# Two dense layers of a graph network in one stage, with part of the rounding on another engine

## The reference

```
edge_feat = gelu((x[src] + edge_attr) @ W_pre + b_pre) * bases
aggr = segment_sum(edge_feat, dst, num_segments=50000)
y = x + aggr
h = relu(batch_norm(y @ W1 + b1, g1, be1))      # mean and variance over all 50000 nodes
h = relu(batch_norm(h @ W2 + b2, g2, be2))
x = layernorm(x + y + h)                         # x + y = 2 (x + aggr / 2)
```

## Time and profile before

| what | value |
|---|---|
| median of 3 runs | 2237.25 us (2236.58 to 2238.08) |
| the profiled execution, its own time | 2248.79 us |
| its span (first to last instruction) | 2247.0 us |
| TensorE, weight loads, VectorE, ScalarE, GpSimd busy | 72%, 58%, 74%, 61%, 58% |
| DMA read and written | 332.27 MB, 295.04 MB, 279 GB/s over the span |
| statistics L500, mean of one | 0.688 us, 392 times |
| relu L780, mean of one | 0.809 us, 196 times |
| weight and instruction queues q8, q14 | 31 and 38 packets, 0.82 MB |

### The profile page before, as it was taken

One profiled execution on the slowest core, in us unless ns is written; L12 is line 12 of the kernel. 1 busy time (PEld: TensorE's weight loads), 2 busy tenths in 40 slices (PEclk: granted clock), 3 DMA queues, 4 the chain that ended last, 5 costly groups with the idle time before them and its releaser, 6 DMA issues. The chain is left out here.

```text
span 2247.0 us, 29418 instructions
## 1 busy us (share of the span) xinstructions
PE 1609.5 (72%) x7554; PEld 1295.5 (58%) x7554; DVE 1666.1 (74%) x3358; ACT 1365.9 (61%) x1981; POOL 1313.1 (58%) x1204
## 2 busy tenths in 40 slices
PE   2645569999996888994333333332599999999994
PEld 2434448888884655663232233232488778888884
DVE  2646646666667888996999999998377667777673
ACT  1322325555775766773888888887266656666663
POOL 5543147770006887001999999999446666666653
PEclk8877879999998999997555555555799999999997
DMA  9999759998879999995999999997412111212110
GB/s 341 368 347 352 260 161 340 342 340 316 289 249 285 342 339 342 344 325 232 385 397 399 401 404 400 395 407 308 169 37 67 63 62 57 65 63 64 55 53 32
DMA packets 171831, 572.69 MB, mean 255 GB/s; under 512 B 27441, under 2 KB 50583, under 8 KB 170322
## 3 DMA queue, kind: packets, MB, share of 16 engines
q1 hardware_dynamic: 123282, 445.99, 52.3%
q0 software_dynamic: 47136, 73.04, 13.8%
q10 hardware_dynamic: 1344, 52.84, 6.3%
HBM read 332.27 MB, written 295.04 MB: 279 GB/s over the span
## 5 line engine op out<-in xcount | busy, mean ns | idle before, releaser
L968 PE MATMUL d_pN<-k_ident,d_r 128*128 128x128 f32 x784 | 191.6, 425 | 337.2 <-ACT d_r L983 336.5
L968 PEld LDWEIGHTS d_pN<-k_ident,d_r 128*128 128x128 f32 x784 | 153.0, 222 | 375.9 <-issue 343.9
L500 DVE BATCH_NORM_STATS2 k_stats<-d_pH 128x512 f32 (+1 forms) x392 | 253.2, 688 | 100.8 <-PE d_pH L52 91.7
L991 ACT ACTIVATE d_o<-d_u,d_nb,d_rs 128x256 f32<-128x256 f32 x392 | 203.6, 590 | 81.2 <-POOL d_nb L1027 81.2
L1034 POOL TENSOR_TENSOR d_u<-d_x,k_base 128x1024 f32<-128x1024 f32 x98 | 230.9, 2356 | 14.6 <-DVE d_x L1059 9.5
L590 POOL DMA_INDIRECT scratch_y<-k_sums,k_target x98 | 151.9, 1550 | 120.7 <-POOLq L61 69.1
L50 PE MATMUL d_pH<-d_r_h,k_w_h 128*128 128x512 f32 x392 | 164.3, 419 | 57.3 <-DVE d_r_l L829 27.5
L780 ACT ACTIVATE d_r<-d_h,d_coef 128x512 f32<-128x512 f32 x196 | 149.2, 809 | 87.0 <-DVE d_r_l L829 41.8
L637 ACT ACTIVATE d_y_h<-d_pT 128x1024 fp32r<-128x1024 f32 x98 | 100.5, 1025 | 157.2 <-PE d_pT L606 133.1
L811 POOL DMA_INDIRECT scratch_y<-k_sums,k_target x98 | 175.0, 1786 | 33.3 <-issue 21.8
L530 POOL TENSOR_TENSOR bn_rstd<-bn_var,k_minus_half 128x2 f32<-128x2 f32 x2 | 1.5, 726 | 318.3 <-DMA d_h<-scratch_h 176.7
(11 more groups left out here) (201 smaller groups left out, 4960.1 us busy)
## 6 DMA issues: line engine op xcount, KB each, us to landing
d_y<-scratch_y SPq DMA_DIRECT2D x196, 512.0 KB
scratch_h<-d_h SPq DMA_DIRECT2D x196, 512.0 KB
d_h<-scratch_h SPq DMA_DIRECT2D x196, 512.0 KB
scratch_y<-in_x ACTq DMA_DIRECT2D x25, 2000.0 KB
scratch_x<-d_x SPq DMA_DIRECT2D x97, 512.0 KB
out<-d_o SPq DMA_DIRECT2D x97, 512.0 KB, 7.7
attr<-in_attr_t SPq DMA_DIRECT2D x25, 512.0 KB, 28.4
bases<-in_bases_t SPq DMA_DIRECT2D x25, 512.0 KB
```

The costliest lines, as they stand in the source:

```text
L500: return dve.bn_stats(out, psum)
L968: last = pe.transpose(pN[b][:, j, cc * P:(cc + 1) * P], r[:, b, cc, j * P:(j + 1) * P], K.ident[:])
L991: last = act.activation(o[:, q, j], u[:, q, j], ACT.Identity, bias=nb[:, q, J + j:J + j + 1], scale=rs[:, q, J + j:J + j + 1])
```

## The change

`dense1` and `dense2` become one stage, `dense12`, without the barrier between them. The passes are numbered g = 0 to 195, the first 98 for layer 1. One ring of four takes the loads of both layers. The last five blocks of layer 1 stay in SBUF (`held`) and are the first of layer 2, so they are neither stored nor loaded; room for them comes from `hid_h`, `hid_l`, `a1h`, `a1l` of `edges0`, which now lie in `e_h` and `e_l`, and from the tiles that the two stages had each for themselves. The second scatter (`take_back`) follows the first on GpSimd: tile t waits until its part of `K.sums` is halved and until the blocks of y that it touches are turned; their number, `passed`, is worked out in `edges0` by five small VectorE operations and goes through DRAM as `need` does. The first 73 tiles stand ahead of layer 1's coefficients in GpSimd's stream, the other 25 behind. In layer 2, for every g divisible by three, ScalarE makes the rounded part right behind the relu, in place of VectorE's cast. SP issues the store of g-3 behind the load for four passes on. The loops are written out.

```
+        begin_i, last_i = sb("begin_i", [S.ET, S.NB], I32), sb("last_i", [S.ET, 1], I32)
...
-        hid_h, hid_l = sb("hid_h", [P, C, P], F32R), sb("hid_l", [P, C, P], F32R)
-        a1, a1h, a1l = sb("a1", [P, P]), sb("a1h", [P, P], F32R), sb("a1l", [P, P], F32R)
+        hid_h, hid_l = e_h[:, :, 0:P], e_l[:, :, 0:P]
+        a1, a1h, a1l = sb("a1", [P, P]), e_h[:, 0, P:2 * P], e_l[:, 0, P:2 * P]
...
+            sp.dma_start(last_i[:], A["tile_last"]).then_inc(index_full, 16)
...
-            sp.wait_ge(need_kept, 16)
+            sp.dma_start(A["passed"].rearrange("(n o) -> n o", o=1), passed[:]).then_inc(need_kept, 16)
+            sp.wait_ge(need_kept, 32)
             sp.dma_start(K.need[:], A["need"].rearrange("(o n) -> o n", o=1)).then_inc(need_kept, 16)
-            sp.wait_ge(need_kept, 32)
+            sp.dma_start(K.passed[:], A["passed"].rearrange("(o n) -> o n", o=1)).then_inc(need_kept, 16)
+            sp.wait_ge(need_kept, 64)
...
+            then(dve.tensor_scalar(out=begin[:], in0=begin_i[:], scalar1=float(S.last_node), scalar2=None, op0=ALU.min))
+            then(dve.tensor_copy(last_dst[:], last_i[:]))
+            then(dve.tensor_scalar(out=begun[:], in0=begin[:], scalar1=last_dst[:, 0:1], scalar2=None, op0=ALU.is_le))
+            then(dve.tensor_reduce(out=passed_f[:], in_=begun[:], axis=mybir.AxisListType.X, op=ALU.add))
+            dve.tensor_copy(passed[:], passed_f[:]).then_inc(need_done, 1)
...
-def dense1(nc, A, K, S):
+def dense12(nc, A, K, S):
...
+        early = ET * 3 // 4
+        HELD = 5
+        passes = [(1, k) for k in range(NB)] + [(2, (NB - HELD + n) % NB) for n in range(NB)]
+        loads = [g for g, (layer, k) in enumerate(passes) if layer == 1 or k < NB - HELD]
+        stores = [g for g, (layer, k) in enumerate(passes) if layer == 2 or k < NB - HELD]
...
+            for g in range(2 * NB + 3):                       # SP
+                if g in load_no and load_no[g] + 4 < len(loads):
+                    load(load_no[g] + 4)
+                if g - 3 in store_no:
+                    store(store_no[g - 3])
...
+            def take_back(t):                                 # GpSimd
+                pool.wait_ge(halved, t // J + 1)
+                passed = pool.value_load(K.passed[0:1, t:t + 1], min_val=1, max_val=NB)
+                pool.wait_ge(turned, passed)
+                pool.sem_inc(row_read, 1)
+                if t >= 4:
+                    pool.wait_ge(halved_in[t % 4], 16 * (t // 4))
+                scatter(t, halved_in)
...
+            for t in range(early):
+                take_back(t)
+            coef_pool(pool)
+            for t in range(early, ET):
+                take_back(t)
...
+            def multiply(g):                                  # TensorE
+                w = 2 if layer2(g) else 1
+                pe.wait_ge(lo_done, g + 1)
+                if g >= 2:
+                    pe.wait_ge(h_done, g - 1)
...
+            def relu(g):                                      # ScalarE
+                if g in load_no:
+                    act.wait_ge(full[load_no[g] % 4], 16 * (load_no[g] // 4 + 1))
+                if g >= NB + 2:
+                    act.wait_ge(lo_done, g - 1)
+                for cc in range(C):
+                    last = act.activation(r[:, g % 2, cc], source(g)[:, cc * B:(cc + 1) * B], ACT.Relu,
+                                          bias=coef[:, 1, cc:cc + 1], scale=coef[:, 0, cc:cc + 1])
+                last.then_inc(relu_done, 1)
+                if hi_on_scalar(g):                           # g % 3 == 0
+                    act.wait_ge(product, g - 1)
+                    act.wait_ge(relu_done, g - NB + 1)
+                    act.activation(part_h[:, g % 2], r[:, g % 2], ACT.Copy).then_inc(hi2_scalar, 1)
...
+                if g >= 8 and g % 3 == 2 and (g - 8) // 3 < S.EB:
+                    halve((g - 8) // 3)
+            act.wait_ge(coef_ready, 1)
+            for g in range(NB, NB + 3):
+                relu(g)
+            for g in range(NB + 1, 2 * NB + 1):
+                if g + 2 < 2 * NB:
+                    relu(g + 2)
+                out(g - 1)
...
+            def parts(g):                                     # VectorE
+                on_scalar = sum(hi_on_scalar(n) for n in range(NB, g + 1))
+                if hi_on_scalar(g):
+                    dve.wait_ge(hi2_scalar, on_scalar)
+                else:
+                    dve.wait_ge(relu_done, g - NB + 1)
+                    dve.wait_ge(product, g - 1)
+                    dve.tensor_copy(part_h[:, g % 2], r[:, g % 2]).then_inc(hi2_vector, 1)
+                    dve.wait_ge(hi2_vector, g + 1 - NB - on_scalar)
+                dve.tensor_tensor(out=part_l[:, g % 2], in0=r[:, g % 2], in1=part_h[:, g % 2].bitcast(F32),
+                                  op=ALU.subtract).then_inc(lo_done, 1)
...
+            for g in range(NB + 1, 2 * NB + 1):
+                stats(g - 1)
+                if g + 1 < 2 * NB:
+                    parts(g + 1)
```

More of the change, by code:

```diff
@@ L550, in dense1 @@
[L550 to L556, removed]
@@ new lines, in dense12 @@
+        landed, halved, row_read = sem("landed"), sem("halved"), sem("row_read")
+        full, stored = [sem(f"full{n}") for n in range(4)], [sem(f"stored{n}") for n in range(4)]
+        turned, relu_done, hi_done, lo_done, product, stats_done, h_done = (
+            sem("turned"), sem("relu"), sem("hi"), sem("lo"), sem("product"), sem("stats"), sem("h_done"))
+        hi2_scalar, hi2_vector = sem("hi2_scalar"), sem("hi2_vector")
+        coef = sb("coef", [P, 2, C])
+        coef_ready, coef_vector, coef_pool = bn_coefficients(sem, sb, K, 0, K.stats, coef, "bn1")
@@ L562, in _, with load, store @@
             rows = node_rows(A["y"], S)
[L564 to L577 removed]
+            def load(n):
+                g = loads[n]
+                layer, k = passes[g]
+                if n >= 4:
+                    before = loads[n - 4]
+                    if layer2(before):
+                        sp.wait_ge(relu_done, before - NB + 1)
+                    else:
+                        sp.wait_ge(turned, before + 1)
+                if layer == 2:
+                    sp.wait_ge(stored[k % 4], 16 * (k // 4 + 1))
+                    got = A["h1"][k]
+                else:
+                    needed = sp.value_load(K.need[0:1, k:k + 1], min_val=1, max_val=ET)
+                    sp.wait_ge(landed, needed)
+                    got = rows(k)
+                sp.dma_start(ring[:, n % 4], got).then_inc(full[n % 4], 16)
+            def store(n):
+                g = stores[n]
+                layer, k = passes[g]
+                sp.wait_ge(h_done, g + 1)
+                sp.dma_start(A["h2" if layer == 2 else "h1"][k], h[:, n % 4]).then_inc(stored[n % 4], 16)
+            for n in range(4):
+                load(n)
+            for g in range(2 * NB + 3):
[3 more added lines that the diff above has]
+                    store(store_no[g - 3])
             for q in range(4):
[L579 removed]
+                sp.wait_ge(stored[q], 16 * ((len(stores) - 1 - q) // 4 + 1))
         @block.gpsimd
@@ L621, in _ @@
-            with pe.Fori(0, loops) as i:
-                for k, q in quarters(i):
-                    turn(k + 1, q + 1 if q < 3 else 0)
-                    multiply(k, q)
-            k = S.NB - 2
-            turn(k + 1, 1)
-            multiply(k, 0)
-            multiply(k + 1, 1)
+            turn(0)
+            for g in range(2 * NB):
+                if not layer2(g + 1):
+                    turn(g + 1)
+                multiply(g)
         @block.scalar
         def _(act):
-            act.sem_inc(h_done, 2)
@@ new lines, in _ @@
+            hi(0)
+            hi(1)
+            for g in range(1, NB + 1):
+                if g + 1 < NB:
+                    hi(g + 1)
+                out(g - 1)
[7 more added lines that the diff above has]
+                    relu(g + 2)
+                out(g - 1)
@@ L854, in _ @@
+            lo(0)
+            lo(1)
+            for g in range(1, NB + 1):
+                stats(g - 1)
+                if g + 1 < NB:
+                    lo(g + 1)
+            dve.wait_ge(stats_done, NB)
+            coef_vector(dve)
+            parts(NB)
+            parts(NB + 1)
+            for g in range(NB + 1, 2 * NB + 1):
+                stats(g - 1)
+                if g + 1 < 2 * NB:
+                    parts(g + 1)
+            dve.wait_ge(stats_done, 2 * NB)
             coef2_vector(dve)
@@ L1611, in laid_out @@
         "tile_first": np.broadcast_to(dst_r[0:S.ET, 0], (S.NB, S.ET)),
+        "tile_last": i["dst"][[min((t + 1) * P, E) - 1 for t in range(S.ET)]].reshape(S.ET, 1),
         "dst_r": dst_r, "before_r": before,
```

313 lines of the change are left out of this document (78 added, 235 removed).

## The result

The changed kernel takes 2310.12 us (median of 4, 2307.20 to 2312.74) beside 2237.58 us for the kernel before on the same chip: a ratio of 1.0324 [1.0307, 1.0342], 72.5 us slower. The profiled execution took 2309.2 us, its span is 2307.4 us.

The account below looks back on a forecast made before the run. Layer 1 bound by the tensor engine; layer 2 by full DMA, then a latency loop with VectorE almost full. 45.6 - 4.6 + 0.7 = +41.7 us on 2237.25 gives 2279; own range 2262 to 2292, stretched to 2312.

Parts of the forecast that it names:

- the signs named ahead: Layer 2: multiplies in threes, one 5.3 us behind the last; ScalarE waiting before 33 roundings; VectorE under 80%; DMA near 0.85.
- late stores and a late GpSimd: Two rivals: layer 1's stores return late, 2299, chance 0.1; GpSimd is late for the coefficients, 2312, chance 0.08.
- three signs of being wrong: No idle in threes, GpSimd's last of the 73 scatters ending after 679, or a clock below 1.00 in layer 2.
- The cycle of a third on ScalarE: Layer 2: rounding and out copy hold the tensor engine once in three blocks; 11.76 us a cycle, layer 2 +45.6 us.
- a rival with +185: Layer 2: the clock falls in the holes, two slow multiplies in each of 32 cycles; 2464 us, chance 0.05.
- No barrier: Between the layers: aggregation can start about 0.1 us after layer 1's last statistics, saving 4.6 us.
- Stage before: Stage ahead of layer 1: two more small DMAs in the chain ahead of the weight loads, +0.7 us.
- Second scatter: GpSimd during layer 1: 73 tiles at 2.06 us end at 663.7, 15.6 us of slack, register loads hidden, cost 0.
- Stores of layer 1: SP queue in layer 1: stores go out 3.0 us later behind the next load, cost 0, at most 41 us.
- Written-out loops: Dense stages: instruction waits from written-out code cost 0 to 19 us, taken as 0.
- Alone it could lift layer 2's first part to the 3.23 us of the second: Layer 2: held blocks and the scatter moved out could bring the first part to 3.23 us a block.
- The difference carried over: Whole kernel: +41.7 us, reckoned on the profiled execution 11.5 us above the median, was added to the median 2237.25.

Follow-up runs that it names:

- experiment 1: The changed kernel with all of layer 2's rounding back on VectorE: 2216.7 us, 0.9902 of the kernel before.
- experiment 2: The changed kernel with ScalarE's order relu, out copy, rounding: 2217.6 us, 0.9908 of the kernel before.
- experiment 3: The changed kernel with eight unused matmuls filling each hole of the tensor engine in layer 2: 2282.0 us, 1.0187 of the kernel before.
- experiment 11: The changed kernel without rounding on ScalarE, its new row of 98 integers padded to 128 elements: 2210.2 us, 0.9882 of the kernel before.
- experiment 5: The kernel before with only TensorE's loop of layer 1 written out: 2248.4 us, 1.0014 of the kernel before.
- experiment 6: The changed kernel without rounding on ScalarE, all 98 tiles of the second scatter behind layer 1's coefficients: 2247.0 us, 1.0001 of the kernel before.
- experiment 12: The changed kernel without rounding on ScalarE and with no blocks kept in SBUF: 2218.6 us, 0.9911 of the kernel before.
- experiment 7: The changed kernel with three buffers for the rounded part, four blocks held, ScalarE's order unchanged: 2241.8 us, 0.9980 of the kernel before.
- experiment 9: The changed kernel with three buffers, four blocks held, and ScalarE's out copy ahead of the rounding: 2212.6 us, 0.9890 of the kernel before.
- experiment 10: The changed kernel with three buffers, out copy ahead of the rounding, and half of the rounding on ScalarE: 2210.2 us, 0.9875 of the kernel before.

## Why the prediction was right, and where its sizes were off

*Direction and place: right.* Slower, in layer 2, by an idle tensor engine once in three blocks. Experiments 1 and 2 show that the edit and its place in ScalarE's order do it. Of the signs named ahead the idle time in threes came (5.21 us for the 5.3 said), the wait ahead of the rounding (32 of 33), VectorE at 66% (under 80 said) and the DMA share lower still, 0.73 for 0.85.

*The time: within the range by luck.* 2310 lies outside the forecast's own 2262 to 2292. It lies within the outer bound of 2312, which was stretched for late stores and a late GpSimd, and neither cost TensorE anything. What brought the time there is the clock, which the range left out, and one of the prediction's three signs of being wrong, a clock below 1.00 in layer 2, did come.

*The cycle of a third on ScalarE: right within 3%.* From rows of another stage and of the scatter's regime it gave 5.30 + 6.46 = 11.76 us. Measured at full clock: 5.21 + 6.28 = 11.49. The two terms that were off: the multiply came 0.09 earlier, and VectorE's chain over two blocks is 6.28, not the 6.46 of the earlier trace rows; its statistics start 3.07 us behind the multiply's start (904.90 - 901.83) and not 3.26. Over 31 cycles that is 8 us less than forecast.

*The clock: the step that was mis-sized.* The prediction had layer 2 at +45.6 with a full clock, and a rival with +185 if it fell in every cycle, chance 0.05. It fell in 20 of 32, for 7 or 8 matmuls of one multiply and not for two whole ones, so the price was 28.8 us (experiment 3). The rival's price per matmul was too high as well: it took the difference of two durations, 0.63 - 0.39 = 0.24, where the starts are only 0.195 further apart. The argument against it, that TensorE kept clock 1.00 at 31.36 of 40 us busy, compared a different pattern: there the idle time came in short waits at every block. Here it is 32.45 of 40 at 0.90, the idle time in one piece of 2.15 us. A share of busy time read off one stretch didn't carry over to another. The Trainium skill, "TensorE: Matmul & The Clock Gate", section "HAM oscillation — how this bites in real kernels", describes waits that recur in every round and slow the matmuls behind each. The trace agrees in part: matmuls behind the hole take 0.63 us (915.12), but behind 20 of 32 holes and not behind all, and the holes are 2.15 us long, where the page's waits are some 3 to 5 us.

*No barrier: right.* -4.7 measured, -4.6 forecast, the engine idle 11.68 us where about 12 was said.

*Stage before: small, off by 1.5.* +2.2 in place of +0.7. Runs with the same code there differ by up to 6 us, so this can't be told from none.

*Layer 1: +3.4 in place of 0.* The pace, 0.03 us a block over 97 steps, makes 3 us of it and comes from where the operands lie (experiment 11; experiments 5 and 6 speak against two other reasons). No view of the trace of before could show it.

*Second scatter: right, with less slack.* GpSimd was done at 675.2, wanted at 685.1: 9.9 us, not 15.6. The pace was 2.08. The prediction has 2.06, but its own rows give (506.0 - 304.1) / 97 = 2.08, which is 1.5 us over 73 tiles. The register loads stayed hidden (409 ns median). Not foreseen: the second scatter starts at 523.81, not at 513.3. The first one's last tile starts 7.5 us later (513.43, not 505.97), so its landing, the last record of this line, comes 8.5 us later, and another 2.0 us pass from there to the first tile:

```profile
L664 POOLq EVENT_SEMAPHORE  x98: 17/17/17, 310.2 to 521.8; - x98
```

*Stores of layer 1: right in the cost, with no room left.* This answers to the earlier trace rows:

```profile
584.31 0.48 PE L50 MATMUL d_pH<-d_part_h,k_w_h 128*128 128x512 f32 x1
...
585.51 1.02 ACT L732 ACTIVATE d_h<-d_pH 128x1024 f32<-128x1024 f32 x1
...
587.98 0.48 PE L50 MATMUL d_pH<-d_part_h,k_w_h 128*128 128x512 f32 x1
...
590.02 0.44 SPq L628 DMA_DIRECT2D scratch_h<-d_h  x1
```

The copy ends at 586.53 and its store goes out at 590.02, 3.5 us later (forecast 3.0). How long these stores (L628) took to land, and what the copies of layer 1 waited for them (us in total, times, longest):

```profile
DMA to landing us min/median/max: 6.3/9.6/11.9
...
ACT d_h L732 <- DMA scratch_h<-d_h: 1.4, 4, 0.7
```

The prediction took a landing of 7.7 us from another stage and reckoned that a buffer is wanted again 10.5 us after its store goes out. The median is 9.6 and the longest is above 10.5: four copies waited, 1.4 us in all. None of it reached TensorE.

*Five blocks in SBUF: right, nothing measurable* (experiment 12). *Written-out loops: right, nothing measurable* on TensorE (experiment 5).

*"Alone it could lift layer 2's first part to the 3.23 us of the second": right, and a little low.* (3.46 - 3.23) x 98 = 22.5 us would be the gain. From its first multiply to the end of its last, layer 2 of experiment 1 takes 311.3 us, 27.4 less than before: its pace is 3.15, below the 3.23. 21.7 of these go with the scatter (experiment 6). That the whole kernel gains 22 is a coincidence of several terms.

*The difference carried over: off by 5 us.* The prediction let the 11.5 us by which before's execution lies above its median stand in both kernels. After's execution lies 0.9 below its median instead, so the spans differ by 60.4 and the medians by 72.5. Of the 11.5 us, 6.9 lie behind layer 2, in code that the change leaves alone, and some 5 ahead of its end; in which stage these are, and why, stays open.

Together: 2279 + 28.8 (clock) - 8 (cycle) + 3.4 (layer 1) + 1.5 (stage before) = 2304.7, and these 5 us make 2310.

## What to carry to other kernels

Work moved from a full engine to one with room is paid where it stands in that engine's queue: an operation that must wait for the end of X may not stand ahead of one that the start of the next X needs. Look for both reasons of such a hole, the order and the buffer; here removing either alone brought back most of the loss, but only with both removed was layer 2 shorter than with no rounding on ScalarE (323.7 and 319.5 us beside 326.1; experiments 2, 7, 9, 10, one profiled execution each, the ratios overlap). A recurring hole is also to be priced with the clock it may cost, and a small new buffer allocated ahead of the operands of the tensor engine is an edit too.

## What was not expected of the hardware

- With a row of 392 bytes allocated ahead of its moving operands a matmul of 512 columns starts every 0.233 us, with the same row padded to 512 bytes every 0.230 (experiments 1 and 12 beside 11): 3.67 and 3.64 us a block.
- The same 2.15 us hole lowers the clock to half in some cycles and not in others: behind 20 of 32 with a hole every 11.5 to 13 us, behind 4 of 16 with a hole every 20.9 us and more. Each time it stayed low for 7 or 8 matmuls.
- With rounding, copies and multiplies well ordered, TensorE reached 156 of 160 us at a DMA share of 0.98 and 342 GB/s (experiment 10).

Experiment 10 has the lowest ratio, 2210.2 us or 0.9875 of before, but isn't told apart from 1, 2, 9, 11 and 12, which are all clear of both kernels. It has the unpadded row; with the padding of experiment 11 it might give some 3 us more, by the difference between 1 and 11, but that wasn't run.
